# A two-layer transformer kernel on Trainium2: the order of one DMA queue, of ScalarE's copies and of a few TensorE steps is changed

## What is computed

```python
x = x + L0_attn(layernorm(x))   # 16 heads of 8, RoPE, causal; a second score
                                # product of q*q and k*k is added (times 0.1);
                                # two attentions (of Q,K and of rotated Q,K) are
                                # combined with a gate
x = x + L0_ffn(layernorm(x))    # relu(x @ W1 + b1) @ W2 + b2, inner width 512
x = x + L1_attn(layernorm(x))   # its own layer norm, 16 heads of 8, not causal
x = x + L1_ffn(layernorm(x))    # silu(x @ Wg.T) * (x @ Wu.T) @ Wd.T, width 384
```

## Time and profile before

| | |
|---|---|
| median of 3 runs (lowest, highest) | 368.12 us (367.98, 368.98) |
| the profiled execution, its whole time | 369.26 us |
| its span, first to last instruction | 367.5 us |
| TensorE matmuls | 304.7 us, 83% of the span |
| VectorE | 254.1 us, 69% |
| ScalarE | 222.9 us, 61% |
| GpSimd | 168.2 us, 46% |
| granted clock of TensorE, mean | 0.944 |

### The profile page before, as it was taken

How to read it: one execution, slowest core, us unless ns; L and a number is a source line. 1 busy time by engine, 2 the same in 40 slices (tenths; PEclk the granted TensorE clock), 3 DMA queues, 4 the chain that set the end, 5 groups by cost and what they waited for, 6 DMA issues and landing times.

```text
span 367.5 us, 8365 instructions
## 1 busy us (share of the span) xinstructions
PE 304.7 (83%) x2832; PEld 217.2 (59%) x2832; DVE 254.1 (69%) x993; ACT 222.9 (61%) x501; POOL 168.2 (46%) x383
## 2 busy tenths in 40 slices
PE   2862678688989997979999999989789999999654
PEld 1651556465757675757777666756556666665443
DVE  5766588787676766666767676669686989884422
ACT  5355265767566765657666766676566676767410
POOL 6253546766567575767776523515041404033020
PEclk9986668998999999999999999999999999999966
DMA  7578022423121104133101011110302010100000
GB/s 206 201 185 196 19 61 70 110 66 102 33 59 44 47 2 133 28 96 66 30 2 31 3 51 24 36 38 4 86 25 67 24 36 24 39 16 2 14 16 14
DMA packets 23034, 21.19 MB, mean 58 GB/s; under 512 B 2896, under 2 KB 20048, under 8 KB 22992
## 3 DMA queue, kind: packets, MB, share of 16 engines
q1 hardware_dynamic: 22992, 20.66, 20.7%
HBM read 13.18 MB, written 7.34 MB: 56 GB/s over the span
## 4 chain that ended last, share of the span: by engine, by line
PE 55%; DVE 16%; POOL 11%; ACT 7%; issue 5%; DMA 3%; SPq 2%; ACTq 0%; POOLq 0%
PE bank L907 11%; DVE NM L709 6%; PE bank L828 4%; PE bank L881 4%; PE bank L937 4%; PE bank L986 4%; PE bank L950 4%; DMA KS<-scr 3%; PE bank L864 3%; PE bank L978 2%; PE bank L862 2%; POOL RS L392 2%; PE bank L865 2%; DVE HG L733 2%; PE bank L814 2%
## 5 line engine op out<-in xcount | busy, mean ns | idle before, releaser
L544 ACT ACTIVATE PB<-bank 128x384 f32<-128x384 f32 (+1 forms) x256 | 136.1, 546 | 82.4 <-PE bank L883 43.8
L709 DVE TENSOR_REDUCE NM<-bank 128x2 f32<-128x512 f32 x128 | 84.9, 685 | 33.3 <-PE bank L865 33.2
L881 PE MATMUL bank<-QS,KS 128*128 128x256 f16 x256 | 70.8, 277 | 4.0 <-ACT PB L544 3.0
L907 PE MATMUL bank<-PB,VP 128*32 128x256 f32 (+1 forms) x1024 | 61.7, 359 | 1.9 <-POOL PB L431 1.2
L704 DVE CUSTOM_DVE_ANT_0 JUNK<-bank,MSF 128x128 bf16<-128x128 f32 x128 | 36.5, 285 | 38.3 <-PE bank L862 38.3
L706 DVE CUSTOM_DVE_ANT_0 JUNK<-bank,MSF 128x256 bf16<-128x256 f32 x128 | 53.7, 420 | 0.0
L907 PEld LDWEIGHTS bank<-PB,VP 128*32 128x32 f32 x1024 | 26.8, 109 | 24.9 <-issue 9.7
L431 POOL TENSOR_SCALAR_AFFINE_SELECT PB<-PB 128x512 f32<-128x512 f32 x64 | 40.6, 634 | 0.0
L458 POOL TENSOR_TENSOR xs<-xs,Y 128x256 f32<-128x256 f32 x8 | 5.8, 726 | 71.1 <-DVE Y L718 71.1
L864 PE MATMUL bank<-KS,QS 96*128 96x256 f16 x128 | 35.3, 276 | 2.9 <-DMA KS<-scr 2.9
L862 PE MATMUL bank<-KS,QS 96*128 96x256 f16 x128 | 36.2, 288 | 0.0
(11 more groups left out here) (90 smaller groups left out, 613.5 us busy)
## 6 DMA issues: line engine op xcount, KB each, us to landing
scr<-PR SPq DMA_DIRECT2D x16, 256.0 KB, 2.9
QS<-scr SPq DMA_DIRECT2D x16, 128.0 KB, 2.8
QS<-scr SPq DMA_DIRECT2D x32, 64.0 KB, 2.9
KS<-scr SPq DMA_DIRECT2D x32, 64.0 KB, 2.9
KS<-scr SPq DMA_DIRECT2D x16, 128.0 KB, 3.1
scr<-PR SPq DMA_DIRECT2D x16, 128.0 KB, 1.9
out_x<-xs SPq DMA_DIRECT2D x8, 128.0 KB, 1.9
W<-in_w SPq DMA_DIRECT2D x1, 576.0 KB, 6.1
```

What stands on the lines that cost most here:

```text
L544: act.activation(PB[:, s % RING, 0:n], TB_[s % 2][:, 0:n], ACT.Exp).then_inc(s_e, 1)
L709: dve.tensor_reduce(m[:, s, 0:2], o[:, :].rearrange("q (n k) -> q n k", n=2), AX.X, ALU.max, negate=True).then_inc(s_mx, 1)
L881: pe.matmul(o[:, 0:S], k[:, 0:P], q[:, :], start=True, stop=True)
L907: ins = pe.matmul(o, v, pr, start=(g % 2 == 0 and kt == 0), stop=True, skip_group_check=True)
```

## The change

Five edits. (1) `store1(b)` stands behind the mid load and `load_max(i + 1, 0)` in every phase, not only for the last sequence. (2) On ScalarE the second `evac_o` and `copy_xT2` come ahead of the exponential of their slot. (3) `dn` goes from slot 12 to 13 and `add_dn` from 13 to 14. (4) For layer 0's last sequence `q1` and `qk1` go from slot 10 to 7, their copies from 10 and 11 to 8. (5) From phase 12 on `mr1` goes from slot 0 to slot 1, and on TensorE the last `pv` stands ahead of it there.

```diff
-         "dn": (2, 12), "add_dn": (2, 13)})
+         "dn": (2, 13), "add_dn": (2, 14)})
-STEP_LAST0 = {"xT2": (3, 7), "copy_xT2": (3, 8), "q1": (4, 10), "qk1": (4, 10), "copy_q1": (4, 10), "copy_k1": (4, 11), "hi1": (4, 13), "lo1": (4, 14)}
+STEP_LAST0 = {"xT2": (3, 7), "copy_xT2": (3, 8), "q1": (4, 7), "qk1": (4, 7), "copy_q1": (4, 8), "copy_k1": (4, 8), "hi1": (4, 13), "lo1": (4, 14)}
-M1 = 0
+def m1_slot(i):
+    return 1 if phase(i - 4)[0] == 1 else 0
...
@@ block.sync
-                L, b = phase(i - 4)
-                if L == 0 and b < B - 1:
-                    store1(b)
                 for (L, b), (j, place_) in LOADS.items():
                     if j == i and place_ == "mid":
                         load_stack(L, b, 0)
                 if i + 1 < NPH:
                     load_max(i + 1, 0)
-                if i == when(0, B - 1) + 4:
-                    store1(B - 1)
+                L, b = phase(i - 4)
+                if L == 0:
+                    store1(b)
                 L, b = phase(i - 2)
                 if L == 1:
                     store_out(b)
...
@@ block.scalar
+                    if s == last_pv_slot(i) + 1 and 0 <= i - 1 < NPH:
+                        evac_o(i - 1, 1)
+                    for b in due(0, "copy_xT2", i, s):
+                        act.wait_ge(*filled("xT2", b))
+                        act.activation(XT[2][b % 2][:, :], psum("xT2", b)[:, 0:S], ACT.Identity, bias=b_col,
+                                       scale=g_col).then_inc(*empties("xT2", b))
                     if 0 <= i < NPH:
                         exp(i, s)
-                    if s == last_pv_slot(i) + 1 and 0 <= i - 1 < NPH:
-                        evac_o(i - 1, 1)
...
-                    if s == M1 and 0 <= i < NPH:
+                    if s == m1_slot(i) and 0 <= i < NPH:
                         row_max(i, 1)
...
-                    for b in due(0, "copy_xT2", i, s):
-                        act.wait_ge(*filled("xT2", b))
-                        act.activation(XT[2][b % 2][:, :], psum("xT2", b)[:, 0:S], ACT.Identity, bias=b_col,
-                                       scale=g_col).then_inc(*empties("xT2", b))
...
@@ block.tensor
                         shifted(i, s)
-                    if s == M1 and 0 <= i < NPH:
+                    if s == last_pv_slot(i) and 0 <= i - 1 < NPH:
+                        pv(i - 1, 3)
+                    if s == m1_slot(i) and 0 <= i < NPH:
                         m = into("mr1", i)
                         for b in due(0, "v1", i, s):
                             project1_v(b, m)
                         max_rows(i, 1, m)
-                    if s == last_pv_slot(i) and 0 <= i - 1 < NPH:
-                        pv(i - 1, 3)
```

More of the change, by code:

```diff
@@ L107, in bank_uses @@
     for i in range(NPH):
-        uses += [(H * (i - 1) + m0_slot(i - 1), 6 if phase(i - 3)[0] == 1 else 7, ("mr0", i)), (H * i + M1, 6, ("mr1", i))]
+        uses += [(H * (i - 1) + m0_slot(i - 1), 6 if phase(i - 3)[0] == 1 else 7, ("mr0", i)), (H * i + m1_slot(i), 6, ("mr1", i))]
         L, b = ORDER[i]
```

## The result

The changed kernel takes 353.4 us (median of 4 executions, 353.08 to 355.51) against 368.55 us (367.98 to 369.64, 4 executions) of the kernel before beside it: ratio 0.959, 95% interval 0.955 to 0.963. A second comparison on another occasion gave 353.29 against 367.78. Forecast were 354.1 us. The span went from 367.5 to 353.8 us with the same 8365 instructions; TensorE is busy for 302.2 us, 85% of it.

A forecast was written before the change was run, and what follows sets the result against it. TensorE was taken to set the pace in phases 2 to 15, SyncE's store holding back the mid load. The terms, 6.4 + 2.6 + 1.1 + 1.4 + 0.85 + 1.7 = 14.05 us, off the median 368.12 gave 354.1; range 351.0 to 359.8.

The forecast's parts named there:

- A: SyncE's queue: with the store behind the mid load, TensorE's four waits for a stack go; 6.4 us, bounds 5.5 to 6.8.
- B: ScalarE, second `evac_o` ahead of the exponential: 0.34 us in phases 2 to 8, 0.25 in phase 9; 2.6 us.
- C: ScalarE, `copy_xT2` ahead of the exponential: 0.05 us in phases 3 to 7, 0.43 and 0.40 in 8 and 9; 1.1 us.
- The tie: Slot 15, phases 3 to 7: `norm1`'s transposes already start just as GpSimd finishes `norm1`, so TensorE would wait there instead.
- D: `dn` in slot 13: slot 14 comes 0.35 us earlier in phases 10, 12, 13 and 14; 1.4 us, bounds 0 to 1.6.
- E: `mr1` in slot 1: three waits of about 0.2 us go, half of phase 15's 0.4; 0.85 us, bounds 0.4 to 1.1.
- F: Last sequence's `q1` in slot 7, phase 11: waits of 0.54 and 0.97 us go; 1.7 us, bounds 0.9 to 2.2.
- R1: Rival: both copies moved on ScalarE buy nothing, absorbed by ties at `relu1` and `norm1`; 357.8 us, chance 18%.
- R2: Rival: the four stack waits return in slot 8, if its 2.5 to 3 us of room is missing; 360.5 us, 10%.
- R4: Rival: slower; the late store makes half 1 miss slot 8 in all eight phases of layer 0's tail; 372 us, 4%.
- R3: Rival: the two moved copies save their whole waits, 0.62 and 0.46 us per phase; 350.1 us, chance 8%.

The follow-up runs named there:

- both ties are untied: The changed kernel with `norm1`'s transposes moved behind the next slot 0's scores and `relu1` ahead of slot 4's exponential: 349.21 us, ratio 0.949 to the kernel before.
- The kernel held back on purpose: The changed kernel with SyncE holding half 1 of the next stacks in phases 5 and 6 until `shifted` of slot 3: 357.02 us against 353.4.

## Why the prediction was right

The time (354.1 for 353.4) and the mechanism came out. Term by term, with what the runs showed:

- **A, 6.4 us.** Between two traces 6.58, on the average of the traces about 5.7. The mechanism is shown by the kernel with edit 1 alone. The 0.2 us that each wait was to cost beyond its length came out at 0.15 to 0.17. What was not seen is that a stack's landing scatters, so one trace of a DMA wait is a sample and not a size. The store's readers cost nothing: TensorE has no stack wait left.
- **B, 2.6 us.** 0.27 a phase and not 0.34, so 7 x 0.27 + 0.25 = 2.1. The step that failed is "`h1` starts at about 130.88", 0.05 us behind `relu1`: after, it follows `relu1`'s end (129.83 + 0.48 = 130.31) by 0.14, and it had done so before as well (131.08 to 131.22). `h1` was bound by `relu1` already, in phases 2 to 8 without a wait of its own in the table of waits, and gained just about what the copy took in the chain (0.25 us). The estimate of 3.8 from the figure of the Trainium skill (ScalarE: Activation LUTs, Rules for kernel authors) is too high; it is stated for an ACTIVATE with its bias by pointer, and this is a COPY without one. The row of the trace, 0.25 us, held.
- **C, 1.1 us.** 0 in phases 3 to 7 (0.05 each were forecast), 0.48 in phase 8 (0.43) and 0.62 in phase 9 (0.40): 1.1 again, by errors that cancel. For phase 9 there is a check free of stack waits: 19.79 us with edit 1 alone and 18.89 in the changed kernel, so B and C together gave 0.90 there. The tie was read right, down to the 0.38 us of the new wait. The small delay of the exponential showed as a wait of 0.20 of line 883, hidden by the tie.
- **D, 1.4 us.** 0.44 in each of phases 12 to 14, and 0.40 more in phase 10 than edit 1 gave there (2.42 - 2.02). But phase 15 lost 0.65, which the prediction did not price: it counted "Four phases (10, 12, 13, 14)" and took the fifth to be untouched. There `dn` in slot 12 had cost nothing; back in it, the 0.65 return. In slot 13 it holds up the shifted scores of slot 14, by 0.64 us in the kernel with edit 3 alone.
- **E, 0.85 us.** 0.19 x 3 = 0.57; the 0.2 counted in phase 15 was not there: in place of the wait of 0.44 for the maximum stands one of 0.47 for an exponential. The prediction's own terms make 3 x 0.2 + 0.2 = 0.8.
- **F, 1.7 us.** 1.99 together with D's part of phase 11; alone only bounded.

These make 6.6 + 2.1 + 1.1 + 1.7 + 0.6 + 2.0 = 14.1 between the two traces; phase 15 takes 0.7 back, and phases 0 and 1 and the drain give 0.3, for a difference of 13.7 in span. That the sum fits so well owes something to errors of both signs: B and E were smaller than forecast, D and F together larger, and phase 15 was left out.

The fit of the time itself is in part luck. With the average of A the same terms come to about 12.8 us, whereas the medians differ by 15.2 in the first comparison and 14.5 in the second. No run here attributes the rest of 1.7 to 2.4 us. The falls of the clock described in the last section are a candidate, not shown.

R1 was half right (C was absorbed in five of seven phases, B was not), R2 and R4 are refused by the measured room, and R3's full gains appear only once both ties are untied: phase 4 is then 16.85 us, 1.04 less than with edit 1 alone, for R3's 0.62 + 0.46.

## What to carry over

When an engine waits for one instruction of another, look at what it needs next before pricing the removal. Here TensorE started two later steps 0.05 and 0.14 us behind the result that they needed, and in those phases neither had a wait in the table. Moving the instruction that stands at such a tie (`norm1`'s transposes, `relu1`) gave 2.1 and 3.3 us, more than moving the copies (2.1 and 1.1). In a queue that one engine issues in order, sort by readiness, and measure how late the last in line may be by delaying it on purpose. A step laid into a later slot for the busy phases should be checked in the phase at the edge of the schedule, where another engine sets the pace.

## What the hardware showed beside this

TensorE's granted clock fell to half in places that differ from run to run. In the kernels with only the copy of `xT2`, only `dn` or only `q1` changed, it fell within 1 us of the end of the stack wait that closes phase 10; in the trace of before and in two others of that queue order it did not. The waits were 2.05, 2.43 and 1.97 us in the three where it fell, and 1.85, 1.92 and 1.84 us in the three where it did not. The same stretch in the trace of before and in that of the `xT2` kernel (columns as above):

```profile
258.40:261.80 3.40, 1.55 (x15) 1.15 (x14) 1.38 (x2) 1.19 (x2) 0.00 (x0) 1.00 0.47 128
```

```profile
258.40:261.80 3.40, 3.40 (x25) 1.47 (x23) 0.80 (x2) 1.46 (x4) 0.00 (x0) 0.50 0.13 33
```

In the second the clock was at its lower level (0.50, 1.2 GHz) after TensorE had idled 2.05 us for the stack, and phase 11 took 20.48 us for 18.91, 1.6 us more. The kernel held back on purpose shows the same behind its waits of 0.4 and 1.8 us in phase 5. In none of the traces with the new queue order and undelayed loads did the clock fall between phase 3 and the drain. In these traces each fall between phase 3 and the drain stood at or behind the end of such a wait, and where it can be read (phase 11 of the `xT2` and `dn` kernels, phase 5 of the one held back) the phase was 1.2 to 2.0 us longer than its waits explain. Whether that is part of what the medians gained cannot be told from single traces, and stays open.
